# Selective scan on one NeuronCore: exponentials of two states in place, decay products 1024 wide

## The reference, cut to what matters

```python
A = -jnp.exp(A_log)                                   # 512 x 16
def step(h, inp):                                     # h: 128 x 512 x 16
    d_t, u_t, B_t, C_t = inp
    dA = jnp.exp(d_t[..., None] * A)
    h = dA * h + (d_t * u_t)[..., None] * B_t[:, None, :]
    y = jnp.einsum('bdn,bn->bd', h, C_t)
    return (h, y)
```

## Time and profile before

| | us |
|---|---|
| median of three runs | 501.42 |
| the runs | 504.26, 498.4, 501.42 |
| the profiled execution | 500.88 |
| its span (first to last instruction) | 499.1 |
| scan in it: first product of POOL to the end of the last `last_state` | 79.83 to 242.38 |

### The profile page before, as it was taken

How to read it: one execution, slowest core, us unless ns; L and a number is a source line. 1 busy time by engine, 2 the same in 40 slices (tenths; PEclk the granted TensorE clock), 3 DMA queues, 4 the chain that set the end, 5 groups by cost and what they waited for, 6 DMA issues and landing times.

```text
span 499.1 us, 11537 instructions
## 1 busy us (share of the span) xinstructions
PE 407.7 (82%) x4148; PEld 336.2 (67%) x4148; DVE 390.9 (78%) x744; ACT 296.5 (59%) x699; POOL 215.5 (43%) x157
## 2 busy tenths in 40 slices
PE   4979961755875848688999999999999999999843
PEld 1435631635674848568788898888888888888632
DVE  0877788995999996997657657977878787887774
ACT  2645996894999987987124435354453535345530
POOL 2400006994879794979142323242332333133101
PEclk9999995795989978997999999999999999999986
DMA  8961454114311151110300000000000000000000
GB/s 290 382 275 66 130 155 137 32 40 99 118 32 33 39 161 45 52 44 22 133 22 2 3 12 1 13 13 8 15 0 21 0 11 11 11 11 0 22 1 22
DMA packets 18658, 30.94 MB, mean 62 GB/s; under 512 B 2112, under 2 KB 11712, under 8 KB 17920
## 3 DMA queue, kind: packets, MB, share of 16 engines
q1 hardware_dynamic: 18624, 30.49, 18.7%
HBM read 24.16 MB, written 6.32 MB: 61 GB/s over the span
## 4 chain that ended last, share of the span: by engine, by line
PE 55%; DVE 18%; ACT 11%; issue 9%; DMA 3%; POOL 1%; DVEq 1%; SPq 1%; POOLq 0%; ACTq 0%
PE ps L445 46%; PE ps L567 5%; DVE reg_b L1355 4%; ACT hc L933 3%; PE ps L681 3%; DVE ps L1348 3%; DMA ud_t<-ud_dram 2%; ACT ps L925 2%; DVE ps L1345 2%; DVE reg_b L1289 1%; DVE reg_b L1242 1%; DMA xw<-x_fm 1%; ACT reg_b L905 1%; ACT reg_b L1029 1%; POOL reg_b L1148 1%
## 5 line engine op out<-in xcount | busy, mean ns | idle before, releaser
L1148 POOL TENSOR_TENSOR reg_b<-reg_c,reg_a 128x1024 f32<-128x1024 f32 x56 | 130.4, 2364 | 59.0 <-DVE reg_c L1294 58.9
L1171 POOL TENSOR_TENSOR reg_b<-reg_b 128x768 f32<-128x768 f32 x32 | 57.9, 1808 | 116.8 <-DVE reg_b L1427 116.8
L445 PE MATMUL ps<-x1T,Mw 128*128 (+1 forms) x768 | 93.1, 278 | 0.7 <-DVE reg_b L1427 0.7
L445 PEld LDWEIGHTS ps<-x1T,Mw 128*128 128x128 f32 x768 | 88.3, 192 | 3.5 <-issue 1.7
L567 PE MATMUL ps<-ident,hc 128*128 128x128 f32 x456 | 72.3, 307 | 17.2 <-ACT hc L933 16.0
L933 ACT ACTIVATE hc<-reg_b,bc 128x512 f32<-128x512 f32 x96 | 69.0, 718 | 17.4 <-PE ps L567 13.2
L567 PEld LDWEIGHTS ps<-ident,hc 128*128 128x128 f32 x456 | 59.1, 159 | 27.4 <-ACT hc L933 24.1
L925 ACT ACTIVATE ps<-reg_b 128x512 f32<-128x512 f32 x112 | 66.0, 593 | 6.9 <-POOL reg_b L1148 5.3
L1355 DVE SCALAR_TENSOR_TENSOR reg_b<-reg_c,bc,ps 128x512 f32<-128x512 f32 x96 | 70.1, 735 | 0.0
L1348 DVE TENSOR_TENSOR ps<-ps,reg_b 128x512 f32<-128x512 f32 x80 | 54.7, 690 | 9.1 <-ACT ps L925 9.0
L1029 ACT ACTIVATE reg_b<-ps,small 128x128 f32<-128x128 f32 x128 | 45.1, 371 | 12.8 <-DVE small L1432 12.8
(11 more groups left out here) (150 smaller groups left out, 714.1 us busy)
## 6 DMA issues: line engine op xcount, KB each, us to landing
reg_a<-a_dram SPq DMA_DIRECT2D x4, 1024.0 KB, 7.9
Mw<-w_o SPq DMA_DIRECT2D x1, 2048.0 KB, 16.0
ud_dram<-reg_b SPq DMA_DIRECT2D x4, 512.0 KB, 4.3
zs_dram<-x1T SPq DMA_DIRECT2D x4, 512.0 KB, 3.7
ud_t<-ud_dram SPq DMA_DIRECT2D x8, 256.0 KB, 3.1
zs_t<-zs_dram SPq DMA_DIRECT2D x8, 256.0 KB, 2.6
xw<-x_fm SPq DMA_DIRECT2D x2, 512.0 KB, 5.9
mring<-w_q SPq DMA_DIRECT2D x4, 256.0 KB, 4.1
```

The lines of the kernel that those rows point to most:

```text
L445: return pe.matmul(o, l, r, start=start, stop=stop)
L1148: pool.tensor_tensor(dA[:, g % RING], delta_r[:, bass.ds(t, 1), :].to_broadcast([P, SA, DI]), Abc[:, g * SA:(g + 1) * SA, :], ALU.mult).th ...
L1171: pool.tensor_tensor(rq[:, g % 2].rearrange("p a c n -> p (a c n)"), pc[:, g % 2].rearrange("p a c n -> p (a c n)"), psn[:, g % 2].rearran ...
```

## The change

The exponential is taken in place in SBUF, of two states (one group of the ring) in one ACT instruction of 1024. DVE's decay product then reads the exponential and the old states, both of them in SBUF, 1024 wide, and writes PSUM; two pairs of PSUM banks alternate. In step 1 the two products of a pair stay single (512 wide). The adds stay single. POOL's ring is freed by DVE's product (`dah_s`), in the last step's second half by `last_state` (`yl_s`), no longer by the exponential. DVE takes over the wait for the last gate eviction before its first step; SP waits for all of `yl_s` before it overwrites `reg_a`.

```diff
             sp.wait_ge(arg_s, AG * (T - 1))
-            sp.wait_ge(da_s, NST * (T - 1))
+            sp.wait_ge(yl_s, NST)
...
-            def decay(t, n):
...
-                act.activation(ps[:, n % RING, :], dA[:, n // SA % RING, n % SA, :], ACT.Exp,
-                               scale=-1.0).then_inc(da_s, 1)
+            def decay_pair(t, g):
+
+                act.wait_ge(arg_s, AG * (t - 1) + g + 1)
+                act.activation(dA[:, g % RING], dA[:, g % RING], ACT.Exp, scale=-1.0).then_inc(da_s, 1)
...
                 for n in range(NST):
-                    decay(t, n)
+                    if n % SA == 0:
+                        decay_pair(t, n // SA)
...
-                need(pool, da_s, NST * (t - 1) + SA * (g + 1 - RING))
+                if isinstance(t, int) and t == T - 1 and g >= RING:
+                    pool.wait_ge(yl_s, SA * (g + 1 - RING))
+                else:
+                    need(pool, dah_s, AG * (t - 1) + g + 1 - RING)
...
-            def state_decay(t, n):
...
-                dve.tensor_tensor(E_n, E_n, H[:, n, :], ALU.mult).then_inc(dah_s, 1)
+            def decay_states(t, g):
+
+                dve.wait_ge(da_s, AG * (t - 1) + g + 1)
+                need(dve, h_s, NST * (t - 1) + SA * (g - 1))
+                two = ps[:, SA * (g % 2):SA * (g % 2) + SA, :]
                 if isinstance(t, int) and t == 1:
...
+                    for i in range(SA):
+                        last = dve.scalar_tensor_tensor(two[:, i, :], dA[:, g % RING, i, :], step_b(0, SA * g + i),
+                                                        step_du(0), ALU.mult, ALU.mult)
+                    last.then_inc(dah_s, 1)
                     return
+                dve.tensor_tensor(two, dA[:, g % RING], H[:, SA * g:SA * g + SA, :], ALU.mult).then_inc(dah_s, 1)
...
-                dve.scalar_tensor_tensor(hc[:, last_slot(n), :], ps[:, n % RING, :], step_b(T - 1, NST + n), H[:, n, :],
+                dve.scalar_tensor_tensor(hc[:, last_slot(n), :], dA[:, n // SA % RING, n % SA, :], step_b(T - 1, NST + n), H[:, n, :],
                                          ALU.mult, ALU.mult).then_inc(yl_s, 1)
...
             def scan_step(t):
-                state_decay(t, 0)
+                decay_states(t, 0)
                 for n in range(NST):
-                    if n < NST - 1:
-                        state_decay(t, n + 1)
                     state_add(t, n)
+                    if n % SA == 0 and n + SA < NST:
+                        decay_states(t, n // SA + 1)
```

More of the change, by code:

```diff
@@ L1163, in _ @@
             scan_step(1)
-            with pool.Fori(2, T) as t:
+            with pool.Fori(2, T - 1) as t:
                 scan_step(t)
+            scan_step(T - 1)
             rstd_of(veps, rstd, ln1, 3 * T, rs1)
@@ L1337, in step_b @@
                 return bc[:, bass.ds(t, 1), n:n + 1].rearrange("p t n -> p (t n)")
-            def state_decay(t, n):
-                dve.wait_ge(da_s, NST * (t - 1) + n + 1)
-                E_n = ps[:, n % RING, :]
+            def decay_states(t, g):
+                dve.wait_ge(da_s, AG * (t - 1) + g + 1)
+                need(dve, h_s, NST * (t - 1) + SA * (g - 1))
+                two = ps[:, SA * (g % 2):SA * (g % 2) + SA, :]
                 if isinstance(t, int) and t == 1:
-                    dve.scalar_tensor_tensor(E_n, E_n, step_b(0, n), step_du(0), ALU.mult,
-                                             ALU.mult).then_inc(dah_s, 1)
+                    for i in range(SA):
+                        last = dve.scalar_tensor_tensor(two[:, i, :], dA[:, g % RING, i, :], step_b(0, SA * g + i),
+                                                        step_du(0), ALU.mult, ALU.mult)
+                    last.then_inc(dah_s, 1)
                     return
-                dve.tensor_tensor(E_n, E_n, H[:, n, :], ALU.mult).then_inc(dah_s, 1)
+                dve.tensor_tensor(two, dA[:, g % RING], H[:, SA * g:SA * g + SA, :], ALU.mult).then_inc(dah_s, 1)
             def state_add(t, n):
-                dve.wait_ge(dah_s, NST * (t - 1) + n + 1)
+                dve.wait_ge(dah_s, AG * (t - 1) + n // SA + 1)
                 if not (isinstance(t, int) and t == 1):
                     dve.wait_ge(hc_s, NST * (t - 2) + n + 2)
-                dve.scalar_tensor_tensor(H[:, n, :], step_du(t), step_b(t, n), ps[:, n % RING, :], ALU.mult,
+                dve.scalar_tensor_tensor(H[:, n, :], step_du(t), step_b(t, n), ps[:, n % (2 * SA), :], ALU.mult,
                                          ALU.add).then_inc(h_s, 1)
@@ L1386, in last_state @@
             def last_state(n):
-                dve.wait_ge(da_s, NST * (T - 2) + n + 1)
+                dve.wait_ge(da_s, AG * (T - 2) + n // SA + 1)
                 dve.wait_ge(hc_s, NST * (T - 3) + n + 2)
                 dve.wait_ge(y_s, NST * (T - 2) + 1 + n + int(n > FRESH) - WRING + 1)
-                dve.scalar_tensor_tensor(hc[:, last_slot(n), :], ps[:, n % RING, :], step_b(T - 1, NST + n), H[:, n, :],
+                dve.scalar_tensor_tensor(hc[:, last_slot(n), :], dA[:, n // SA % RING, n % SA, :], step_b(T - 1, NST + n), H[:, n, :],
                                          ALU.mult, ALU.mult).then_inc(yl_s, 1)
@@ L1415, in scan_step @@
                         norm1(t - 1)
+            dve.wait_ge(act_free, freed[("Z", CI - 1)][1])
             scan_step(1)
```

## The result

The changed kernel takes 552.11 us (550.19 to 553.38) against 501.5 (498.4 to 504.26) for the kernel before: a ratio of 1.1008, 95% interval 1.0933 to 1.1082. The forecast was 543, the range 522 to 564. The profiled execution took 551.19 us, with a span of 549.4.

A forecast was written before the change was run, and what follows sets the result against it. DVE sets the scan's pace, ACT close behind, POOL some 3 us spare a step. Exclusive use of 196.2 us plus 4.2 and 3.3 made the scan +41.2; with +0.9 for the table load, +42.1 on 500.88 gives 543, range 522 to 564.

The forecast's parts named there:

- The two SBUF operands: Scan: a DVE product with two SBUF inputs and a POOL product exclude each other for their whole length; the deciding term.
- Pair and exclusive sum: Scan: POOL's 2.325 plus DVE's 1.13 make 3.46 us a pair, 27.6 a step; exclusive use sums to 196.2 us.
- the times in which neither product runs: Scan, added to exclusive use: 4.2 us for two DVE stalls on a late load, 3.3 for POOL's reciprocal roots.
- POOL's root: POOL's reciprocal root in the scan: charged 0.55 us, six times, 3.3 us.
- ACT's order: ACT's in-order queue: exponential behind two weighings, 2.28 us in a pair of 3.46, so covered at no cost.
- the stalls behind `ud_t`: Steps 2 and 5: DVE's stalls on the late load shrink from 5.17 and 3.85 to 2.8 and 1.4 us.
- The ring: POOL waits for DVE's product four groups back, not ACT's exponential; in a full exclusive queue, nothing more.
- The load after the scan: Rotation tables, loaded after the scan, now wait for the last `last_state`: +0.9 us, all on the path.
- The wide product, +0.07 us a pair: DVE's 1024-wide products in the scan, 1.13 us start to start: taken alone save 0.07 a pair, 2.8 us over 40.
- No exclusion: Rival: DVE's two-SBUF-input product runs at 1.13 us beside POOL, so 500.5 us, no change; chance 0.11.
- POOL first each time: Rival: POOL always takes the turn until its ring is full, 3.90 us a pair, 561 us; chance 0.14.
- ACT's order without exclusion: Rival: ACT's queue becomes the bound, some pairs 2.9 us against DVE's 2.43, giving 506 us; chance 0.05.

The follow-up runs named there:

- experiment 1: Changed kernel with DVE's decay products reading their own PSUM banks instead of the exponentials in SBUF (minimum for product): 506.91 us, ratio 1.0144.
- (2): Kernel before, its DVE product of steps 2 to 6 reading delta*u in SBUF instead of the exponential in PSUM (minimum for product): 549.55 us, ratio 1.0991.
- Experiment 9: Changed kernel with each exponential issued one pair earlier in ACT's queue: 545.24 us, ratio 1.0873.
- experiment 8: The kernel of experiment 1 with each exponential issued one pair earlier in ACT's queue: 503.35 us, ratio 1.0035.
- (4): Kernel before with only the ring's release changed: POOL waits for DVE's product (last step's second half: last states), not the exponential: 501.1 us, ratio 1.0001.
- experiment 7: Changed kernel with POOL's reciprocal root of each step moved behind the first product of the next step: 557.17 us, ratio 1.1119.
- experiment 5: Changed kernel with each POOL product of 1024 split into two of 512: 546.72 us, ratio 1.0908.
- experiment 10: Changed kernel with POOL's reciprocal root of each step moved behind the second product of the next step: 546.98 us, ratio 1.0918.

## Why the prediction was right, and what it missed

*The two SBUF operands*: right, and now shown from both sides. Take that operand away and 45 of the 51 us go (1); put it alone into the kernel before and 49 come (2).

*Pair and exclusive sum*: the sum is right within 3%, 196.2 us of exclusive use forecast, 190.4 covered by the records. With POOL's 2.325 us a product kept, DVE's turn costs 0.98 where it was taken as 1.13, so a pair in POOL's full queue takes 3.30 us and not 3.46. That error made the forecast's miss smaller, not larger. The steps were to be near 27.6 us and take 28.8 to 30.2.

*The mis-sized term is the times in which neither product runs*: 4.2 + 3.3 = 7.5 us forecast, 21.8 measured. With the smaller exclusive sum, 14.3 - 5.8 = 8.5 us make up the whole difference between the scan's +41.2 and +49.7. Two readings failed in it:

- POOL's root was charged its own 0.55 us, six times. What it costs is the stretch from DVE's last wide product to POOL's next one, as the root waits for the statistic behind an addition and POOL's products wait behind the root: 2.1 to 2.2 us at the end of each of six steps, 12.9 in all. In the kernel before the same wait (2.80 us in the earlier trace rows) lay in POOL's spare time. Once POOL's queue is part of the bound, everything that stands in it is.
- "Two weighings and a wide exponential are 2.28 us in a pair of 3.46, so that is covered" was wrong for ACT's order. An average rate covers nothing when the queue stands for something else: an exponential is late when the weighing ahead of it waits for DVE's addition or for PE, as at 250.75 below. Experiment 9 gives back 3 to 7 us, experiment 8 3.6 to 4.4 where nothing excludes.

The weighings of the changed kernel as a group, and the one behind which the exponential came 0.95 us late for DVE's product of 252.66:

```profile
L923 ACT ACTIVATE hc<-reg_b,bc 128x512 f32<-128x512 f32 x96 | 67.1, 718 | 59.6 <-DVE reg_b L1353 48.5 <-PE ps L567 11.0
```
```profile
250.75 0.72 ACT L923 ACTIVATE hc<-reg_b,bc 128x512 f32<-128x512 f32 x1 [1.76 <-PE ps L567]
```

Forecast and found otherwise: the stalls behind `ud_t`. PE still waits for that load, but step 5, which has one, takes the same 30.2 us as step 6, which has none; the step with the other (33.2) is 3 us longer than that. In steps 2 and 5 DVE also waits for an exponential, as it does in step 6; how much of that wait comes from the late load, no run here separates.

*The ring*: right for the change as it stands (4); experiment 7 shows the point where it begins to cost, POOL a product further ahead.

*The load after the scan*: +0.9 forecast, 257.2 - 256.7 = +0.5 found for everything behind the scan.

*The wide product, +0.07 us a pair*: its length was right (1218 to 1231 ns wherever nothing shuts it out), and the next instruction starts 1.14 us behind it (257.26 to 258.40) where 1.13 was forecast.

*The rivals.* No exclusion is out by 1 and 2. POOL first each time is out by the longest wait of one product and by steps of 28.8 to 30.2, not 31; experiment 7 does have 31.1, by its full ring, so the sign that the forecast named for this rival (steps of 31 us and a full ring) does not prove it. ACT's order without exclusion gave 506 in the forecast and 506.9 in experiment 1. That the two agree so closely is in part luck, as experiment 8 puts down only 3.6 to 4.4 of these 6.4 us to that order; but that much of it was there underneath the exclusion.

## What to carry to other kernels

Before an operand moves from PSUM to SBUF, list the wide SBUF inputs of each DVE instruction and ask what POOL reads meanwhile: with two inputs, a long POOL product and the DVE instruction add up instead of overlapping, and the profile shows it as longer records, not as idle time. Where two engines have become one queue, count every wait in either queue that stood in spare time before, roots, statistics and late inputs alike; here the time in which neither product ran came to 21.8 us where 7.5 were charged. Width alone is worth little (0.07 us a pair, an estimate from the distances between starts) beside what it does to the buffers.

## What was not expected

- A DVE product that waits has the next turn, in all 40 wide products of the changed kernel and all 40 of experiment 5: the longest wait is one POOL instruction, 2.2 us with 1024 elements and 1.1 with 512, although POOL's next product was at hand in the middle of a step.
- It goes the other way for the smallest instruction as well. POOL's root of 128 x 1 takes 0.55 us, and 1.53 at 169.22 of experiment 5 and at 200.22 of experiment 10, where a wide product of DVE had begun shortly before.
- Equal sums by different means: strict handover through the semaphore (experiment 10, 3.63 us a pair) and turns at the operands with an idle stretch per step (28.8 us in eight pairs, 3.6 each) come out within 0.6 us a step.
